# A recommendation tower on one Trainium2 core: the first period gathered in one go, its layer 0 around the second half's turning, the next period's turning one unit earlier

## The reference

```python
def _L0_rec_ref(embeddings, W0, W1, W2):
    x0 = embeddings
    xk = x0
    outs = []
    for W in (W0, W1, W2):
        xk = jax.nn.relu(jnp.einsum('bmd,bhd,mhk->bkd', x0, xk, W))
        outs.append(jnp.sum(xk, axis=2))
    return jnp.concatenate(outs, axis=1)
e = jnp.stack([tbl_0[ids[:, 0]], ..., tbl_31[ids[:, 31]]], axis=1)     # (1024, 32, 16)
z = _L0_rec_ref(e, L0_rec_W0, L0_rec_W1, L0_rec_W2)                    # (1024, 192)
h = jnp.concatenate([z, dense_ctx], axis=1)
h = jnp.maximum(h @ W_top1 + b_top1, 0.0)
h = jnp.maximum(h @ W_top2 + b_top2, 0.0)
y = h @ W_top3
```

## Time and profile before

| | |
|---|---|
| runs | 641.11, 641.93, 644.91 us |
| profiled execution | 639.03 us, its span 637.2 us |
| PE busy | 584.5 us (92%), 3034 instructions |
| DVE busy | 581.5 us (91%), 347 |
| ACT busy | 371.2 us (58%) |
| POOL busy | 443.3 us (70%) |
| granted clock of TensorE, mean | 0.989 of full |

### The profile page before, as it was taken

The page is one execution under the profiler, slowest core; times in us unless marked ns, Lnnn a source line. Parts: engine busy times, 40 slices in busy tenths (PEclk is TensorE's granted clock), DMA queues, the critical chain, the costliest instruction groups (busy, mean ns, idle before and its releaser), DMA issues.

```text
span 637.2 us, 8234 instructions
## 1 busy us (share of the span) xinstructions
PE 584.5 (92%) x3034; PEld 219.8 (34%) x3034; DVE 581.5 (91%) x347; ACT 371.2 (58%) x641; POOL 443.3 (70%) x416
## 2 busy tenths in 40 slices
PE   0578889699898989999999999999999999999998
PEld 0134533133232323333334323333334323334355
DVE  2159986998999999999999999999999999999995
ACT  1037472946756565757666575747676575737551
POOL 5577787798888878886989688886989582703012
PEclk9879999999999999999999999999999999999999
DMA  5661989958294755739282856648391947500000
GB/s 172 183 186 19 303 196 314 278 142 287 70 235 163 205 203 125 284 70 339 45 285 83 199 209 143 266 91 317 58 312 44 228 177 180 231 0 1 0 1 1
DMA packets 33364, 105.85 MB, mean 166 GB/s; under 512 B 8998, under 2 KB 16172, under 8 KB 29484
## 3 DMA queue, kind: packets, MB, share of 16 engines
q1 hardware_dynamic: 24044, 102.72, 51.1%
q0 software_dynamic: 8192, 2.11, 2.4%
q10 hardware_dynamic: 1088, 0.49, 0.4%
HBM read 89.56 MB, written 15.73 MB: 165 GB/s over the span
## 4 chain that ended last, share of the span: by engine, by line
DVE 49%; PE 33%; issue 12%; POOL 2%; ACT 2%; DMA 1%; DVEq 1%; ACTq 0%; POOLq 0%
DVE prod L637 49%; PE accb L758 9%; PE acca L758 9%; PE acc L699 3%; PE acca L783 3%; POOL emb L470 2%; PE spread L805 2%; PE accb L783 1%; PE acc L783 1%; DMA emb<-in_table,idx 1%; PE acc L729 1%; PE accb L706 1%; PE spread L800 1%; DVEq L626 0%; PE acc L720 0%
## 5 line engine op out<-in xcount | busy, mean ns | idle before, releaser
L470 POOL DMA_INDIRECT emb<-in_table,idx x256 | 245.0, 957 | 82.3 <-issue 68.0
L758 PE MATMUL acca<-prod,w 128*64 128x512 f32 x960 | 215.0, 594 | 4.1 <-DVE prod L637 3.3
L758 PE MATMUL accb<-prod,w 128*64 128x512 f32 x896 | 201.6, 596 | 15.5 <-DVE prod L637 15.5
L637 DVE TENSOR_TENSOR prod<-rows,x1a 128x2048 f32<-128x2048 f32 x64 | 145.6, 2279 | 9.9 <-ACT x1a L913 3.1
L637 DVE TENSOR_TENSOR prod<-rows,x2a 128x2048 f32<-128x2048 f32 x64 | 145.5, 2279 | 5.6 <-ACT x2a L959 4.9
L637 DVE TENSOR_TENSOR prod<-rows,x1b 128x2048 f32<-128x2048 f32 (+1 forms) x65 | 145.6, 2246 | 2.0 <-PE accb L758 1.4
L637 DVE TENSOR_TENSOR prod<-rows,x2b 128x2048 f32<-128x2048 f32 x64 | 145.5, 2279 | 0.0
L758 PEld LDWEIGHTS acca<-prod,w 128*64 128x64 f32 x960 | 67.2, 137 | 137.1 <-issue 127.1
L758 PEld LDWEIGHTS accb<-prod,w 128*64 128x64 f32 x896 | 61.5, 137 | 148.3 <-issue 105.9
L488 POOL TENSOR_TENSOR prod<-rows,mates 128x1024 f32<-128x1024 f32 x42 | 99.2, 2381 | 6.4 <-DMA rows<-field_dram 6.2
L959 ACT ACTIVATE x1a<-acc 64x512 f32<-64x512 f32 x58 | 33.1, 570 | 93.6 <-PE acc L699 92.9
(11 more groups left out here) (105 smaller groups left out, 368.9 us busy)
## 6 DMA issues: line engine op xcount, KB each, us to landing
rows<-field_dram SPq DMA_DIRECT2D x30, 2048.0 KB, 14.5
field_dram<-zb_field SPq DMA_DIRECT2D x30, 256.0 KB
mates<-field_dram SPq DMA_DIRECT2D x15, 512.0 KB, 4.5
across<-field_dram SPq DMA_DIRECT2D x56, 128.0 KB
emb<-in_table,idx POOLq DMA_INDIRECT x256
field_dram<-zb_field SPq DMA_DIRECT2D x30, 128.0 KB
rows<-field_dram SPq DMA_DIRECT2D x4, 768.0 KB, 7.4
field_dram<-zb_field SPq DMA_DIRECT2D x15, 192.0 KB
```

What stands on the lines that cost most here:

```text
L470: pool.indirect_dma_start(out=emb[q % EMBS][:, j * EMB:(j + 1) * EMB], out_offset=None, in_=table, in_offset=bass.IndirectOffsetOnAxis(ap= ...
L637: nc.vector.tensor_tensor(prod[:, n % RING, t:t + count, :], of_rows, xs, ALU.mult).then_inc(s_prod, 1)
L758: mm = nc.tensor.matmul(acc[j % 2][side * HID:(side + 1) * HID, :], (w1 if layer == 1 else w2)[:, step, :], prod[:, (made(layer, s, half, ...
```

## The change

Five edits:

- POOL issues all 16 gathers of period 0 without waiting for the first turning. So that each half can still be waited for by itself, the first 8 gathers count on a semaphore of their own, `s_gather_first`; the later waits on the buffer's own semaphore count 8 gathers less.
- On PE the second half's turning moves from ahead of layer 0 to between its second and third step.
- The two matmuls of `keep_busy` behind that turning are removed.
- POOL's wait ahead of period 2's gathers is for five layer 0 steps, the first half's, and not for ten (`steps_before(1)` is 10, `STEPS0` is 5).
- The turning of period 2 moves from behind the sixteenth unit to ahead of it.

```diff
--- before.py
+++ after.py
@@ -283,7 +283,7 @@
         s_x2 = [sem(f"s_x2{n}") for n in "ab"]
         s_z1, s_z2, s_z3 = sem("s_z1"), sem("s_z2"), sem("s_z3")
         s_eight, s_four, s_pair = sem("s_eight"), sem("s_four"), sem("s_pair")
-        s_z1a, s_listed_first = sem("s_z1a"), [sem(f"s_listed_first{h}") for h in range(SPLITS)]
+        s_z1a, s_gather_first, s_listed_first = sem("s_z1a"), sem("s_gather_first"), [sem(f"s_listed_first{h}") for h in range(SPLITS)]
         s_za, s_zb, s_zc = sem("s_za"), sem("s_zb"), sem("s_zc")
         s_tower, s_act, s_y = sem("s_tower"), sem("s_act"), sem("s_y")
         s_wide, s_ones = sem("s_wide"), sem("s_ones")
@@ -470,7 +470,7 @@
                     pool.indirect_dma_start(
                         out=emb[q % EMBS][:, j * EMB:(j + 1) * EMB], out_offset=None, in_=table,
                         in_offset=bass.IndirectOffsetOnAxis(ap=idx[:, q, j:j + 1], axis=0)
-                    ).then_inc(s_gather[q % EMBS], 16)
+                    ).then_inc(s_gather_first if (q, j // FIRST_GATHERS) == (0, 0) else s_gather[q % EMBS], 16)
 
             def gather_early(q):
                 for first, count, pairs in stretches(q):
@@ -517,12 +517,11 @@
 
             pool.wait_ge(s_at, 1)
             gather(0, 0, FIRST_GATHERS)
-            pool.wait_ge(s_turned, 1)
             gather(0, FIRST_GATHERS, FIRST_GATHERS)
             pool.wait_ge(s_turned, SPLITS)
             pool.wait_ge(s_at, 2)
             gather_early(1)
-            pool.wait_ge(s_l0, steps_before(1))
+            pool.wait_ge(s_l0, STEPS0)
             gather_early(2)
             gather_early(3)
             gather(3, 10, 2)
@@ -676,7 +675,7 @@
 
                 pe.wait_ge(s_field, turned_by(q - 1))
                 wait_for(pe, s_act, towers)
-                pe.wait_ge(s_gather[q % EMBS], (q // EMBS + 1) * GATHERS * 16)
+                pe.wait_ge(s_gather[q % EMBS], ((q // EMBS + 1) * GATHERS - (q % EMBS == 0) * FIRST_GATHERS) * 16)
                 by_d = emb[q % EMBS][:, :].rearrange("b (n d) -> b d n", d=DH)
                 for d in range(DH):
                     part = slice(d % QUAD * FIELDS, (d % QUAD + 1) * FIELDS)
@@ -686,7 +685,7 @@
 
             def turn_first(h):
                 wait_for(pe, s_field, h)
-                pe.wait_ge(s_gather[0], (h + 1) * FIRST_GATHERS * 16)
+                pe.wait_ge(s_gather[0] if h else s_gather_first, FIRST_GATHERS * 16)
                 half = emb[0][:, h * FIRST_GATHERS * EMB:(h + 1) * FIRST_GATHERS * EMB]
                 by_d = half.rearrange("b (n d) -> b d n", d=QUAD)
                 for d in range(QUAD):
@@ -844,11 +843,11 @@
 
             pe.wait_ge(s_w12, 32)
             keep_busy(acc[1][:, :], 6)
-            turn_first(1)
-            keep_busy(acc[1][:, :], 2)
             pe.wait_ge(s_w0sum, 3)
             for k in range(EARLY):
                 layer0_first(k, 0)
+                if k == 1:
+                    turn_first(1)
             for i, unit in enumerate(FIRST_UNITS):
                 outer_alone(*unit)
                 if i == 2 * UNITS - 1:
@@ -856,7 +855,8 @@
                         layer0_first(k, 1)
                 if i == 3 * UNITS - 1:
                     turn_fields(1, 0)
-            turn_fields(2, 0)
+                if i == len(FIRST_UNITS) - 2:
+                    turn_fields(2, 0)
             for k in order0(1):
                 layer0(k, 1)
```

## The result

The changed kernel takes 638.35 us (median of 16 runs, 634.92 to 641.00) against 641.45 for the kernel before (16 runs, 638.54 to 644.91): the ratio is 0.9948, with an interval of 0.9930 to 0.9966. It is 3.1 us faster, where 4.7 were forecast. The profiled execution shows less, 638.23 us against 639.03, spans of 636.4 and 637.2, and the reason for that is part of what follows. All spans are read to 0.1 us.

What follows compares the result with a forecast made beforehand. DVE's products were taken as the bound once the pipeline is full, so an earlier start reaches the end. Terms: -5.65 + 0.7 + 0.25 = -4.7 us, from a median of 641.93 to 637.2 us; range 635.2 to 640.8.

Steps and rivals of the forecast that it cites:

- the six cases: The forecast, 637.2 us, and five rivals: 640.3, 639.4 and 636.3 inside the range, 645.4 and 641.9 outside it.
- What bounds the kernel: From 180 us DVE runs through its products; a change ahead of that reaches the end one for one if others keep up.
- Term 1: Start of the kernel: gather 16 ends 2.1 us earlier without POOL's pause and is taken to land at 28.2 us.
- Term 2: Layer 0 steps ahead of the second turning: ACT's x1a starts at 31.95 and not at 37.60 us, 5.65 us earlier.
- Term 3: PE's first four units after the removed busy-work: they start at half clock, at a price of 0.7 us (0 to 1.0).
- Term 4: Period 2's turning, moved ahead of unit 16: PE waits 0.2 to 0.3 us for gather 48, counted in full.
- Gathers behind the rows: Rival at period 2's turning: gather 48 comes only with the row traffic's end, PE waits 3.3 us, 640.3 us; chance 0.14.
- Clock stays down: Rival on PE: half clock lasts through the four units and on, until about 58 us; 3.5 us slower, 645.4 us; chance 0.05.

## Why the prediction was right, and where its sizes were off

The time came out 1.15 us above the forecast and inside the range, but the range holds four of the six cases that the prediction lists, so the time alone does not tell them apart. The marks do, and two signs of being wrong that the prediction named were there in the profiled execution: the second turning at 29.32, later than 29, and PE's wait of 1.31 us at period 2's turning, over 1. The first is scatter, with a mean of 28.6. The second is not: in the six profiles of the table with the turning in its new place the wait is 0 to 1.96 us, 1.27 in the mean.

- **What bounds the kernel.** Right. After slot 3 the kernels run alike; a lead won before DVE resumes reaches the end, but slot 3 itself may take some of it.
- **Term 1, gathers without the pause.** The step, taking the 4.8 us of before over to the earlier issue and not the end of the traffic, was right: 2.1 us over fourteen profiles. The forecast start of 28.2 is 0.4 early for the mean of 28.6 and 1.1 for the profiled execution after.
- **Term 2, x1a.** -5.65 forecast, -4.55 in the profile after, -4.7 for the mean of six profiles against the one before. The second profile with the order of before, the one with slot 3's busy-work, has x1a at 38.65, and against the mean of the two it is -5.2. ACT's listings (to 33.00) and layer 0 (to 32.8) did end together, as forecast, both later by the turning's 1.1 us. The 1.15 us that were to come from POOL's shorter wait ahead of period 2 came with the earlier end of layer 0 on PE; the edit at POOL by itself does nothing (39.2 us either way).
- **Term 3, the missing busy-work.** +0.7 forecast, +0.93 in the profile after and +0.57 in the mean of five (-0.17 to +1.30). In the profile after the clock rose at 42.3, 5.3 us after the units' start; 4.8 was taken, and the five lie between 3.1 and 6.1. The working has the clock of before fall at about 25.8; by the row at 25.50 it had fallen by 25.6, which changes no term.
- **Term 4, period 2's turning.** +0.25 forecast, **+1.16** measured: the term that was mis-sized most. The mechanism was named, with unit 16 and layer 0 behind it; PE and gather 48 were both late by the same 1.3 us, at 74.96 and 70.52, but the landing took 5.75 us to be seen, and 4.7 was taken from one gather of the kernel before. That gather's landing was never seen, as PE came to it at 80.46. It was set by a count of packets, which does not tell whose they are, and gathers 49 to 51 were issued before 77 too. In the changed kernel the same count reached 1536 at 75.5, and PE saw gather 48 at 76.27. The profile without row traffic (1.44 us) and the one with the turning back (35.03) show cause and price. Here the trace decides against what I drew from the Trainium skill, "DMA: Bandwidth & Descriptors", section "Queues, rings and completion order": engines that serve their queues in turn did not bring the gathers out soon (5.75 us against 1.44 without the row traffic). How they share their time between the queues is not shown.
- **The sum.** -4.55 + 0.93 + 1.16 = -2.46 in the profile; with slot 3's 1.66, -0.8. The medians say -3.1. What the runs add to the -2.46 is the scatter of the early marks, and how often the clock falls in slot 3 in either kernel, which the profiles are too few to count. So that the median came within 1.15 us of the forecast is in part luck: slot 3, which the prediction has at nothing, took between 0 and 4.7 us.
- **The rivals.** "Gathers behind the rows" was the nearest: a wait of 1.31 us, between the forecast's 0.25 and its 3.3. "Clock stays down" did not occur; the rise took 5.3 us. That the clock may fall a second time, in slot 3, was no rival of the list.

## What to carry to other kernels

A small transfer that is waited for should be issued before a large one starts, or its landing be costed at what it takes within the traffic (here 4.7 to 6.3 us for 1.4). When a step on a queue is moved forward, ask whether what it waits for moves as far: the turning came earlier by more than its gathers, and cost what stood behind it. And when a kernel's runs spread, look for the idle gaps of PE that end in work which others wait for: two matmuls of busy-work in one such gap were worth 1.2 us here, with nothing behind it that waited for a late gather; what is left of it where something does was not measured.

## What the runs showed of the hardware that was not expected

- The granted clock is lost after short idling, and not each time: in slot 3 after 3.7 us in the changed kernel (at 114.0, PE having started again at 113.8) and not in the kernel before, at the same place of the program; with that gap filled, after 2.46 us (at 123.7, PE having started again at 122.3). It came back 3.6 us after PE had taken up work there in the changed kernel, 4.8 us after in the profile with the gap filled.
- The price in slot 3 is 1.66 to 1.7 us in the three profiles in which the clock is at half once, for 3.4 us (the changed kernel, with slot 3's busy-work, with the rows held back), and 4.2 to 4.7 in the three in which it is at half twice, for 6.8 and 3.4 us (the pause, POOL's wait and the order put back). In those three it had fallen 0.7 to 1.6 us before PE took up the units. What decides when it falls was not followed up.
- A gather of 128 rows of 64 bytes is seen to have landed 1.4 us after POOL has ended it on quiet DMA engines, 4.7 to 6.3 us beside the row transfers of the first half (up to 768 KB each), and 5.5 to 5.8 us beside those of 2 MB.
